# Attention with softmax sums by accumulating transfers: GpSimd's partial sum joins the DMAs' sum, and the sum pass moves back

## The reference, cut to what matters

```python
xn = layernorm(x)                                   # x: 4 x 2048 x 512, fp32
q = split_heads(xn @ q_w.T + q_b) / sqrt(32)        # 16 heads of 32
k = split_heads(xn @ k_w.T + k_b)
v = split_heads(xn @ v_w.T + v_b)
attn = softmax(q @ k^T)                             # per head 2048 x 2048
out = x + (attn @ v) @ out_w.T + out_b + tanh(xn @ w @ a1 @ a2 + ffn_b)
```

## Time and profile before

| | |
|---|---|
| median of 3 runs | 4234.54 us (4233.6 to 4237.1) |
| profiled execution | 4234.31 us, span 4232.5 us |
| PE busy | 4144.6 us, 98% |
| PE weight loads | 2528.2 us, 60% |
| DVE busy | 2932.1 us, 69% |
| ACT busy | 2359.9 us, 56% |
| POOL busy | 3189.9 us, 75% |
| mean granted clock | 0.989 |
| accumulating transfers | 320 of 1024 KB, 335.56 MB, 41.3% of 16 DMA engines' span |

### The profile page before, as it was taken

The page is one execution under the profiler, slowest core; times in us unless marked ns, Lnnn a source line. Parts: engine busy times, 40 slices in busy tenths (PEclk is TensorE's granted clock), DMA queues, the critical chain, the costliest instruction groups (busy, mean ns, idle before and its releaser), DMA issues.

```text
span 4232.5 us, 77485 instructions
## 1 busy us (share of the span) xinstructions
PE 4144.6 (98%) x21728; PEld 2528.2 (60%) x21728; DVE 2932.1 (69%) x4928; ACT 2359.9 (56%) x4517; POOL 3189.9 (75%) x1119
## 2 busy tenths in 40 slices
PE   7999999999999999999999999999999999999999
PEld 5888888655555555555555555555555555555467
DVE  4344334488877777888877888887788888787334
ACT  2222122156666666666666666666666666666621
POOL 0322232269999999999999999999999999999820
PEclk9999999889999999999999999999999999999999
DMA  4444445447777677777777777777777777777677
GB/s 157 149 165 165 156 145 169 152 96 153 161 152 159 148 156 153 158 159 158 157 153 156 156 156 161 154 155 153 159 153 154 162 160 158 151 156 151 151 242 253
DMA packets 268271, 673.36 MB, mean 159 GB/s; under 512 B 109056, under 2 KB 110080, under 8 KB 214656
## 3 DMA queue, kind: packets, MB, share of 16 engines
q0 software_dynamic: 46080, 335.56, 41.3%
q1 hardware_dynamic: 138784, 220.26, 15.8%
q10 hardware_dynamic: 83040, 113.01, 9.5%
HBM read 195.30 MB, written 137.36 MB: 79 GB/s over the span
## 4 chain that ended last, share of the span: by engine, by line
PE 55%; DMA 9%; issue 7%; POOL 6%; ACT 3%; DVE 1%; POOLq 0%; ACTq 0%; SPq 0%; DVEq 0%
PE pv_bank L860 17%; PE sm_bank L838 16%; PE st_bank L854 16%; POOL pool_sum L642 5%; DMA dma_sum<-probs 5%; DMA q_stack<-max_row 3%; ACT probs L696 3%; PE sm_bank L200 2%; PE sm_bank L860 2%; DVE part_max L774 1%; PE st_bank L200 1%; DMA q_stack<-s_ctx 0%; PE sm_bank L847 0%; POOL dma_sum L653 0%; DVE max_row L758 0%
## 5 line engine op out<-in xcount | busy, mean ns | idle before, releaser
L774 DVE TENSOR_REDUCE part_max<-sm_bank 128x1 f32<-128x512 f32 x4096 | 2498.6, 679 | 576.1 <-PE sm_bank L838 576.0
L642 POOL TENSOR_TENSOR pool_sum<-pool_sum,probs 128x2048 f32<-128x2048 f32 x512 | 2461.4, 4807 | 21.8 <-ACT probs L696 6.3
L696 ACT ACTIVATE probs<-st_bank 128x512 f32<-128x512 f32 x3840 | 1958.3, 614 | 602.1 <-PE st_bank L854 560.7
L838 PE MATMUL sm_bank<-k_stack,q_stack 96*128 96x512 f32 x4096 | 1687.5, 416 | 11.4 <-DVEq L752 9.4
L854 PE MATMUL st_bank<-q_stack,k_stack 97*128 97x512 f32 x4096 | 1647.7, 403 | 37.8 <-DMA q_stack<-max_row 19.3
L838 PEld LDWEIGHTS sm_bank<-k_stack,q_stack 96*128 96x128 f32 x4096 | 785.0, 192 | 543.4 <-DVE part_max L774 331.0
L854 PEld LDWEIGHTS st_bank<-q_stack,k_stack 97*128 97x128 f32 x4096 | 777.3, 190 | 321.9 <-ACT probs L696 141.5
L860 PE MATMUL pv_bank<-probs,v_pair 128*32 128x512 f32 x7680 | 935.4, 602 | 0.0
L860 PEld LDWEIGHTS pv_bank<-probs,v_pair 128*32 128x32 f32 x7680 | 204.7, 109 | 455.5 <-ACT probs L696 259.1
L653 POOL DMA_DIRECT2D dma_sum<-probs x320 | 300.3, 938 | 149.9 <-DMA dma_sum<-probs 141.2
L312 POOL TENSOR_TENSOR y_out<-y_out,x_in 128x512 f32<-128x512 f32 x64 | 82.7, 1292 | 370.7 <-ACT y_out L341 364.7
(11 more groups left out here) (88 smaller groups left out, 2328.7 us busy)
## 6 DMA issues: line engine op xcount, KB each, us to landing
dma_sum<-probs POOLq DMA_DIRECT2D x320, 1024.0 KB, 8.6
q_stack<-s_q_hi ACTq DMA_DIRECT2D x122, 256.0 KB, 6.2
k_stack<-s_k_hi ACTq DMA_DIRECT2D x122, 256.0 KB, 5.0
x_in<-in_x SPq DMA_DIRECT2D x16, 1024.0 KB, 7.8
s_q_hi<-qk_hi SPq DMA_DIRECT2D x16, 1024.0 KB, 4.3
s_q_lo<-qk_lo SPq DMA_DIRECT2D x16, 1024.0 KB, 6.4
s_k_hi<-qk_hi SPq DMA_DIRECT2D x16, 1024.0 KB, 4.3
s_k_lo<-qk_lo SPq DMA_DIRECT2D x16, 1024.0 KB, 6.4
```

Of the source, the lines that this page charges most:

```text
L642: nc.gpsimd.tensor_tensor(total[:], one[:], tile_at(r, kt)[:], ALU.add).then_inc(pool_added, 1)
L696: nc.scalar.activation(tile_at(r, kt)[:, q * BLK:(q + 1) * BLK], st_bank[:, st_place(kt * QB + q)], ACT.Exp, scale=SCALE).then_inc(probs_r ...
L774: nc.vector.tensor_reduce(part_max[:, k:k + 1], sm_bank[:, sm_place(k)], AX.X, ALU.max).then_inc(max_scores_read, 1)
L838: nc.tensor.matmul(sm_bank[:, sm_place(k)], q_st[r][0:ROWS, q * P:(q + 1) * P], k_st[r][0:ROWS, b * BLK:(b + 1) * BLK], start=True, stop=T ...
```

## The change

POOL's sum is added onto `dma_sum` by a sixth accumulating transfer (`merge`): it waits for the last addition and for join 5 of its head, and is issued behind addition 0 of the next head. PE makes one sum pass instead of two, and waits for six landings. `CUT` 10 and `SUM_UNIT` 56 put that pass behind the fifth pair of the next head. `RECIP_UNIT` 4 counts in the following head's maxima: the reciprocal stands behind unit 4 of head h+3 and DVE's program is cut into `begin` (units 0 to 7) and `rest`. Join 1 is issued ahead of addition 0, joins 2 to 5 behind additions 1, 3, 5, 7, the scaling ahead of addition 8. A join now names its own tile among its waits. The landing counts are kept apart for even and odd heads (`joined[r % 2]`, `landed`). The head loads stand behind tiles 10 to 15. `heads` gets a second register copy of the head number, for PE alone. SP's program is as it was.

```diff
--- before.py
+++ after.py
@@ -36,19 +36,20 @@
 PER_TILE = UNITS // KT
 AHEAD = 4
 TURN_UNIT = 8
-SUM_UNIT = 40
-RECIP_UNIT = 56
-CUT = 6
-LOAD_AT = [6, 7, 9, 10, 12, 13, 15]
+SUM_UNIT = 56
+RECIP_UNIT = 4
+CUT = 10
+LOAD_AT = [10, 11, 12, 13, 14, 15, 15]
 
 
 CHAINS = [[0, 2, 5, 8, 10, 13]]
+MERGE_AFTER = 0
 POOL_TILES = [kt for kt in range(KT) if not any(kt in tiles for tiles in CHAINS)]
 POOL_ADDS = len(POOL_TILES) - 1
-JOINED = [(len(tiles) - 1) * DMA for tiles in CHAINS]
-JOIN_AFTER = {0: (0, 1), 2: (0, 2), 4: (0, 3), 6: (0, 4), 7: (0, 5)}
+JOINED = len(CHAINS[0]) * DMA
+JOIN_AFTER = {1: 2, 3: 3, 5: 4, 7: 5}
 SLOT = {kt: i % 7 for i, kt in enumerate([*range(1, 13), 14, 15])} | {13: 7}
-SCALE_ADD = 7
+SCALE_ADD = 8
 RESULT_TILES = [9, 11]
 PACK = SEQ // P
 
@@ -523,8 +525,11 @@
 
         def tile_at(r, kt):
 
-            starts = [tiles[0] for tiles in CHAINS]
-            return dma_sum[starts.index(kt)][r % 2] if kt in starts else probs[SLOT[kt]]
+            return dma_sum[r % 2] if kt == CHAINS[0][0] else probs[SLOT[kt]]
+        def landed(h, j):
+            return (h // 2) * JOINED + j * DMA
 
         block = own.enter_context(nc.Block())
 
@@ -641,17 +646,24 @@
                     pool.wait_ge(pool_added, PRIME + h * POOL_ADDS + i)
                 nc.gpsimd.tensor_tensor(total[:], one[:], tile_at(r, kt)[:], ALU.add).then_inc(pool_added, 1)
 
-            def join(h, r, c, j):
+            def join(h, r, j):
+                pool.wait_ge(probs_ready, PRIME + h * UNITS + QB * (CHAINS[0][j] + 1))
                 if j == 1:
-                    pool.wait_ge(tile_used, PRIME + h * KT + CHAINS[c][0] + 1)
-                if j > 1 or not (isinstance(h, int) and h == 0):
-                    pool.wait_ge(joined[c], h * JOINED[c] + (j - 1) * DMA)
+                    pool.wait_ge(tile_used, PRIME + h * KT + CHAINS[0][0] + 1)
+                if j > 1 or not (isinstance(h, int) and h < 2):
+                    pool.wait_ge(joined[r % 2], landed(h, j - 1))
                 pool.sem_inc(join_due, 1)
-                nc.gpsimd.dma_start(dma_sum[c][r % 2][:], tile_at(r, CHAINS[c][j])[:],
-                                    accum_op=ALU.add).then_inc(joined[c], DMA)
+                nc.gpsimd.dma_start(dma_sum[r % 2][:], tile_at(r, CHAINS[0][j])[:],
+                                    accum_op=ALU.add).then_inc(joined[r % 2], DMA)
+            def merge(h, r):
+                pool.wait_ge(pool_added, PRIME + h * POOL_ADDS + POOL_ADDS)
+                pool.wait_ge(joined[r % 2], landed(h, len(CHAINS[0]) - 1))
+                pool.sem_inc(join_due, 1)
+                nc.gpsimd.dma_start(dma_sum[r % 2][:], pool_sum[r % 2][:], accum_op=ALU.add).then_inc(joined[r % 2], DMA)
 
             def scale(h, r):
                 pool.wait_ge(pv_copied, PRIME + h + 1)
@@ -660,9 +672,11 @@
                 nc.gpsimd.tensor_tensor(ctx_out[r % 2][:], pv_copy[r % 2][:], ratio[:], ALU.mult).then_inc(context_ready, 1)
 
             def sum_up(h, r, i):
+                if i == 0:
+                    join(h, r, 1)
                 add(h, r, i)
                 if i in JOIN_AFTER:
-                    join(h, r, *JOIN_AFTER[i])
+                    join(h, r, JOIN_AFTER[i])
 
             for i in range(POOL_ADDS):
                 sum_up(0, 0, i)
@@ -673,6 +687,8 @@
                         scale(h, r)
                     if more >= 1:
                         sum_up(following, (r + 1) % GROUP, i)
+                    if i == MERGE_AFTER:
+                        merge(h, r)
 
             heads(pool, body)
 
@@ -690,8 +706,8 @@
                         if old in POOL_TILES:
                             act.wait_ge(pool_added, PRIME + h * POOL_ADDS - back * POOL_ADDS + adds_after(old))
                         elif old != kt and not (back and isinstance(h, int) and h == 0):
-                            c = [old in tiles for tiles in CHAINS].index(True)
-                            act.wait_ge(joined[c], h * JOINED[c] - back * JOINED[c] + CHAINS[c].index(old) * DMA)
+                            before, place = (h - 1, (r + 1) % 2) if back else (h, r % 2)
+                            act.wait_ge(joined[place], landed(before, CHAINS[0].index(old)))
                     act.wait_ge(scores_ready, h * UNITS + kt * QB + q + 1)
                     nc.scalar.activation(tile_at(r, kt)[:, q * BLK:(q + 1) * BLK],
                                          st_bank[:, st_place(kt * QB + q)], ACT.Exp,
@@ -726,8 +742,9 @@
             def body(h, r, more, following):
                 for kt in range(CUT, KT):
                     exps(h, r, kt)
-                    if kt in LOAD_AT and more >= GROUP - 1:
-                        load(h + GROUP - 1, (r + GROUP - 1) % GROUP, LOAD_AT.index(kt))
+                    for i, at in enumerate(LOAD_AT):
+                        if at == kt and more >= GROUP - 1:
+                            load(h + GROUP - 1, (r + GROUP - 1) % GROUP, i)
                 if more:
                     for kt in range(CUT):
                         exps(following, (r + 1) % GROUP, kt)
@@ -762,26 +779,37 @@
                 dve.wait_ge(sums_loaded, h * DMA + DMA)
                 nc.vector.reciprocal(ratio_col[:], sums_col[:]).then_inc(recip_ready, 1)
 
-            def maxima(s, units=True, old=True, new=True):
-                for k in range(UNITS):
-                    if k == TURN_UNIT and new:
-                        negate(s - 1)
+            def maxima(s, k):
+                if k == 0:
+                    dve.wait_ge(row_max_ready, PRIME + s)
+                dve.wait_ge(max_scores_ready, s * UNITS + k + 1)
+                nc.vector.tensor_reduce(part_max[:, k:k + 1], sm_bank[:, sm_place(k)], AX.X,
+                                        ALU.max).then_inc(max_scores_read, 1)
+            def begin(s, units=True, sums_of=None):
+                for k in range(TURN_UNIT):
                     if units:
-                        if k == 0:
-                            dve.wait_ge(row_max_ready, PRIME + s)
-                        dve.wait_ge(max_scores_ready, s * UNITS + k + 1)
-                        nc.vector.tensor_reduce(part_max[:, k:k + 1], sm_bank[:, sm_place(k)], AX.X,
-                                                ALU.max).then_inc(max_scores_read, 1)
-                    if k == RECIP_UNIT and old:
-                        recip(s - 2)
+                        maxima(s, k)
+                    if k == RECIP_UNIT and sums_of is not None:
+                        recip(sums_of)
+            def rest(s, units=True, new=True):
+                if new:
+                    negate(s - 1)
                 if units:
+                    for k in range(TURN_UNIT, UNITS):
+                        maxima(s, k)
                     dve.wait_ge(max_scores_read, PRIME + s * UNITS + UNITS)
                     nc.vector.tensor_reduce(row_max[:], part_max[:].rearrange("p (q b) -> p q b", b=QB), AX.X,
                                             ALU.max).then_inc(row_max_ready, 1)
 
-            maxima(0, old=False, new=False)
-            maxima(1, old=False)
+            begin(0)
+            rest(0, new=False)
+            begin(1)
+            rest(1)
+            begin(2)
 
             def low(n, par):
                 dve.wait_ge(hi_ready, n + 1)
@@ -876,11 +905,8 @@
 
                 if more >= 2:
                     pe.wait_ge(max_scores_read, PRIME + h * UNITS + 2 * UNITS + sm_before("sum")[0] + 1)
-                for c in range(len(CHAINS)):
-                    pe.wait_ge(joined[c], h * JOINED[c] + JOINED[c])
-                    spread(sum_bank, ones[:], dma_sum[c][r % 2], c == 0, False)
-                pe.wait_ge(pool_added, PRIME + h * POOL_ADDS + POOL_ADDS)
-                spread(sum_bank, ones[:], pool_sum[r % 2], False, True).then_inc(sums_ready, 1)
+                pe.wait_ge(joined[r % 2], landed(h, len(CHAINS[0])))
+                spread(sum_bank, ones[:], dma_sum[r % 2], True, True).then_inc(sums_ready, 1)
 
             def both_scores(h, r, kt, following, more):
 
@@ -909,17 +935,17 @@
                     use(0, 0, 2 * p - 2)
                     use(0, 0, 2 * p - 1)
 
-            def body(h, r, more, following):
+            def body(h, r, more, following, to_turn):
                 r1 = (r + 1) % GROUP
                 for p in range(CUT // 2, KT // 2):
-                    both_scores(h, r, 2 * p, following, more)
-                    both_scores(h, r, 2 * p + 1, following, more)
+                    both_scores(h, r, 2 * p, to_turn, more)
+                    both_scores(h, r, 2 * p + 1, to_turn, more)
                     use(h, r, 2 * p - 2)
                     use(h, r, 2 * p - 1)
                 if more >= 1:
                     for p in range(CUT // 2):
-                        both_scores(following, r1, 2 * p, following + 1, more - 1)
-                        both_scores(following, r1, 2 * p + 1, following + 1, more - 1)
```

(19 more changed lines are left out.)

## The result

The changed kernel takes 4769.7 us (median of 4, 4764.5 to 4789.5) against 4235.8 us; ratio 1.127, 95% interval 1.1235 to 1.1302. It is slower by 534 us, three times as much as forecast and outside the range.

The account below looks back on a forecast made before the run. PE was taken as the bound, held at times by the row's landing. A late row would lengthen heads from 49.36 to 52.2 us, +176 over 62 heads, +2 at the end: 4234.3 + 178 = 4412 us, range 4270 to 4580.

Parts of the forecast that it names:

- One pass less: On PE, one sum pass fewer per head saves 0.85 us, alone worth 54 us.
- The sixth transfer: On POOL, one more issue of at most 0.88 us; merge landing costs nothing, or 1 to 3 us per head if POOL is late.
- The row is ready: Row of maxima ready for SP to issue at t = 42.5, with sums stored at 30.7.
- The ratio stored 9.2 behind it: On SP, 9.2 us from store of sums to store of the ratio, at t = 39.9.
- The small transfer lands with the join: On the DMA engines, a small transfer lands with the join shadowing it; the row 0.3 us behind join 4, at 52.2.
- rival 1: PE's clock falls too in each head's stop, 2.4 us more: head 54.6 us, time 4561 us; chance 0.27.
- the ratio's landing: In SP's queue, ratio stored at 39.9 lands with join 3, so broadcasts start from about t = 41.7.
- the broadcasts: In SP's queue, four broadcasts ahead of the row take 2.1 us to issue, leaving SP free at about t = 43.8.
- The row's landing: Row issued behind join 4 lands at t = 52.2; PE needs it at 47.94 and stands still 4.3 us per head.
- Rival 2: Row lands before t = 47.9, so POOL's 48.1 us per head is the bound: 4156 us; chance 0.11.
- Rivals 3 and 4: Row only a little late, 4230 to 4305, chance 0.10; PE waits for merge or DVE's sums, 4280, chance 0.05.

Follow-up runs that it names:

- Row first: Changed kernel with SP issuing the row of maxima ahead of waiting for the ratio and of its four broadcasts: 4180.6 us, ratio 0.987 to the kernel before.
- the run without the merge: Changed kernel with the row issued ahead of the ratio's wait and broadcasts, but no sixth transfer and two sum passes at the new place: 4223 and 4230 us.
- 36 added matmuls: Changed kernel with 36 extra, thrown-away matmuls of PE in front of each head's first score: 4698 us.
- the head loads back: Changed kernel with the head loads at their old tiles 6, 7, 9, 10, 12, 13 and 15, SP's queue untouched: 4608.8 us.
- join 4 small: Changed kernel with join 4 cut to 32 of its 2048 columns: 4395 us.
- the small join 3: Changed kernel with join 3 cut to 32 columns: 4519 us.

## Why the prediction was wrong

The cause, the place and the sign were right; three terms of the sum for the head were too small. Steps, by the prediction's own list:
- One pass less is worth 0.85 us. Row first is 54 us faster than before, and 64 x 0.85 = 54, but that the two agree is partly luck: PE's wait for the row went (0.3 us per head) and one for the merge came (0.4), and the run without the merge puts the merge and its pass together at 46.
- The sixth transfer was to cost POOL at most 0.88 us: its record takes 1.2 in the changed kernel, and it is hidden there. Its landing holds PE 0.4 us per head in the row-first kernel; I had 0 or 1 to 3.
- The row is ready 11.8 us behind the store: right. The ratio stored 9.2 behind it: 9.4 (9.2 in the mean).
- The small transfer lands with the join: right in kind, shown by the small joins. But the row lands 2.4 us behind join 4 in the mean (4.2 in the head shown) and not 0.3, and always just behind the last of the broadcasts issued ahead of it, which the prediction had not taken into the landing.
- **Mis-sized, first term: the clock.** The forecast summed the head at full clock, that is, put the fall of the clock at nothing, and set it beside as rival 1, with 2.4 us. It came on top: the stop is 6.7 us in this head and 9.2 at its end, as long as the one of the earlier trace rows or longer, and 12 matmuls behind it take 2032.65 - 2027.37 = 5.28 us, 0.44 each. The sums are stored at 33.1 and not 30.7.
- **Second term: the ratio's landing.** I took 1.8 us, join 3 being issued 1.0 us behind the store of sums (31.7 less 30.7) and the ratio landing as it lands. Join 3 is issued 1.7 behind the store in the mean, lands in 9.9, and the ratio lands 1.5 (median) behind it: 3.9 us in the mean. The clock has no part in this, since it moves the store and join 3 alike: with 36 added matmuls and the full clock the ratio still takes 4.0.
- **Third term: the broadcasts.** I took 2.1 us; their issue takes 3.5 in the mean, 4.4 here. With the head loads back it is 1.9, with join 4 small 2.1, so both are behind it.
- The row's landing, 8.4 forecast (52.2 less 43.8): 8.3. The figure is right by luck. It was to be issued 2.0 us behind join 4 (43.8 less 41.8) and to land 0.3 behind it; it is issued 4.5 behind and lands 2.4 behind, and the two errors cancel.

Together: 52.2 + 2.4 + (3.9 - 1.8) + (3.5 - 2.1) = 58.1 us, which is the head that was measured. Then 62 x (58.1 - 49.36) = 542, of 534 to 538 that were measured. The sum is made from measured terms, so it shows where the time went and is no forecast. What a run shows of each alone: the clock, by the added matmuls (2.6 us on the row's landing), the ratio's landing, by the small join 3 (1.8 us instead of 3.9), the broadcasts, by the loads back (1.9 instead of 3.5). The range took in the clock or the bounds of the row's landing, one at a time, and never the ratio's landing or the broadcasts; its top should have been the sum of the upper ends.

Rival 1 came, and with it the two terms that it lacked: 4561 by its sum. Rival 2 (the row in time) is what the row-first kernel shows, by another order in the queue: forecast 4156, measured 4181. Rivals 3 and 4 didn't come.

## What to carry to other kernels

When a step is moved in time, go through the queue that carries its results, in its program order, and ask what stands behind each wait: the change touched no line of SP's program and cost 534 us by way of its queue, and one reordering turned it into a gain of 54. And where a chain has several uncertain terms, sum their upper ends for the top of the range, since they can all come at once. A wait that costs nothing should be priced in its new place before it is moved: the merge 5.5 us earlier cost 262 us.

## What the runs showed of the hardware

- A stop of PE of 5.9 to 9.2 us in each head left the array at its lower level (granted clock 0.50, 0.44 us per matmul of 512 columns, 1.2 GHz) for about 5 us after the stop at 2027.37, and for over 9 us after the one at 2087.38; with 24 useless matmuls in the stop the kernel ran 86 us faster.
- The row, an 8 KB transfer, took 1.8 to 10.9 us to land over all runs, depending on what was in flight: with a 1 MB accumulating transfer taken out of its way the median fell from 8.3 to 3.9, and it was 2.0 in 20 heads of row first without the merge, where no accumulating transfer was in flight at its issue.
- SP's issue itself gets slow: in the changed kernel the same four broadcasts took 1.8 us to issue in one head and up to 4.6 in another, with joins and head loads in flight.
